# Heads and state written channel-major in column tiles: a Mamba block with a four-bit FFN on one core

## What is computed

```python
# u (16, 256, 256); all float32
z, xBC, dt = split(u @ W_in, [512, 1280])          # W_in (256, 1288)
xBC = silu(conv(xBC))                              # causal, 4 taps along the sequence, with bias
x, B, C = split(xBC, [512, 640])                   # x: 8 heads of 64 channels; state 128
dt = softplus(dt + dt_bias); A = -exp(A_log)       # one of each per head
y = ssd(x * dt, A * dt, B, C)                      # y_t = sum over s <= t of
                                                   #   exp(sum of A*dt over (s, t]) (C_t . B_s) dt_s x_s
y = (y + x * D) * silu(z)
y = y * rsqrt(mean(y^2) + 1e-5) * norm_scale
h = layernorm(u + y @ W_out)
g, v = h @ Wg.T, h @ Wu.T                          # 256 -> 2048, four-bit weights with a scale
out = layernorm(h + (gelu_tanh(g) * v) @ Wd.T)     # per 32 inputs; 2048 -> 256
```

## Time and profile before

| | |
|---|---|
| runs | 974.57, 980.9, 981.12 us; median 980.9 |
| profiled execution | 978.1 us, its span 976.4 us |
| mean granted TensorE clock | 0.969 of full speed |
| PE busy | 912.1 us (93%) |
| PEld busy | 795.8 us (82%) |
| DVE busy | 689.8 us (71%) |
| ACT busy | 528.8 us (54%) |
| POOL busy | 84.3 us (9%) |
| DMA | 23.28 MB, queues busy for 7.4% of 16 engines |

### The profile page before, as it was taken

One profiled execution on the slowest core, in us unless ns is written; L12 is line 12 of the kernel. 1 busy time (PEld: TensorE's weight loads), 2 busy tenths in 40 slices (PEclk: granted clock), 3 DMA queues, 4 the chain that ended last, 5 costly groups with the idle time before them and its releaser, 6 DMA issues.

```text
span 976.4 us, 16131 instructions
## 1 busy us (share of the span) xinstructions
PE 912.1 (93%) x5416; PEld 795.8 (82%) x5416; DVE 689.8 (71%) x1402; ACT 528.8 (54%) x1044; POOL 84.3 (9%) x170
## 2 busy tenths in 40 slices
PE   4678689899999999999999999999999999999997
PEld 3447679788897888878897889878898888888887
DVE  6766987786668775687658765687668775776453
ACT  4643477447634764447634664448645664455232
POOL 2110001200020001200021001200011001100000
PEclk9787879999999999999999999999999999999999
DMA  4011100010001000010001000010001000000000
GB/s 132 31 57 48 32 17 22 15 41 1 23 1 66 0 0 21 22 43 0 21 0 65 0 0 21 21 45 0 21 0 65 1 1 12 35 21 1 1 34 11
DMA packets 18813, 23.28 MB, mean 24 GB/s; under 512 B 1728, under 2 KB 15296, under 8 KB 18752
## 3 DMA queue, kind: packets, MB, share of 16 engines
q1 hardware_dynamic: 18176, 22.56, 7.1%
q10 hardware_dynamic: 576, 0.03, 0.0%
HBM read 14.19 MB, written 4.19 MB: 19 GB/s over the span
## 4 chain that ended last, share of the span: by engine, by line
issue 54%; PE 29%; DVE 8%; POOL 4%; ACT 2%; DMA 1%; POOLq 0%; DVEq 0%; SPq 0%; ACTq 0%
PE mixer L561 2%; PE up_bank L481 2%; PE down L481 2%; PE down L482 2%; PE down L483 2%; PE up_bank L483 2%; PE up_bank L482 2%; PE gate_bank L481 2%; PE gate_bank L483 2%; PE gate_bank L482 2%; DVE xbc L897 2%; PE mixer L481 2%; PE mixer L482 1%; PE mixer L483 1%; POOL rms L1131 1%
## 5 line engine op out<-in xcount | busy, mean ns | idle before, releaser
L481 PE MATMUL down<-wd_hi,in_hi 128*128 128x256 f32 x512 | 145.2, 284 | 0.7 <-DVE in_lo L1018 0.7
L482 PE MATMUL down<-wd_lo,in_hi 128*128 128x256 f32 x512 | 144.6, 282 | 0.0
L483 PE MATMUL down<-wd_hi,in_lo 128*128 128x256 f32 x512 | 144.3, 282 | 0.0
L897 DVE SCALAR_TENSOR_TENSOR xbc<-mixer,chan,xbc 128x510 f32<-128x510 f32 (+1 forms) x162 | 111.1, 686 | 28.3 <-ACT xbc L689 23.4
L767 ACT ACTIVATE act_sb<-gate_bank 128x512 f32<-128x512 f32 (+1 forms) x144 | 78.8, 547 | 82.7 <-PE gate_bank L483 81.5
L753 ACT ACTIVATE in_hi<-act_sb 128x512 fp32r<-128x512 f32 (+1 forms) x144 | 83.4, 579 | 68.9 <-PE down L483 55.6
L481 PE MATMUL up_bank<-hT_hi,wu_hi 128*128 128x512 f32 (+1 forms) x288 | 109.1, 379 | 11.1 <-DVE act_sb L1032 11.0
L481 PE MATMUL gate_bank<-hT_hi,wg_hi 128*128 128x512 f32 (+1 forms) x288 | 115.2, 400 | 4.5 <-DVE wg_lo L1085 4.5
L1032 DVE SCALAR_TENSOR_TENSOR act_sb<-up_bank,act_sb 128x512 f32<-128x512 f32 (+1 forms) x144 | 90.6, 629 | 37.6 <-PE up_bank L483 20.1
L483 PE MATMUL gate_bank<-hT_hi,wg_lo 128*128 128x512 f32 (+1 forms) x288 | 108.2, 376 | 0.0
L482 PE MATMUL gate_bank<-hT_lo,wg_hi 128*128 128x512 f32 (+1 forms) x288 | 107.6, 374 | 0.0
(11 more groups left out here) (205 smaller groups left out, 2008.5 us busy)
## 6 DMA issues: line engine op xcount, KB each, us to landing
xbc<-in_u_t_dram SPq DMA_DIRECT2D x7, 512.0 KB, 3.6
h_sb<-in_u_dram SPq DMA_DIRECT2D x7, 512.0 KB, 4.0
h_res<-h_sb SPq DMA_DIRECT2D x7, 512.0 KB, 3.4
out_dram<-h_res SPq DMA_DIRECT2D x7, 512.0 KB, 3.3
scales<-in_ffn_s_dram SPq DMA_DIRECT2D x24, 128.0 KB, 2.0
packed<-in_ffn_w_dram SPq DMA_DIRECT2D x8, 96.0 KB, 1.9
xbc<-in_u_t_dram SPq DMA_DIRECT2D x2, 256.0 KB, 2.7
xbc<-in_W_in_dram SPq DMA_DIRECT2D x1, 512.0 KB, 5.8
```

What stands on the lines that cost most here:

```text
L481: nc.tensor.matmul(dst, lh, rh, start=first, stop=False, skip_group_check=True)
L482: nc.tensor.matmul(dst, lh, rl, start=False, stop=False, skip_group_check=True)
L483: return nc.tensor.matmul(dst, ll, rh, start=False, stop=last, skip_group_check=True)
L897: ins = stt(acc[:, :, d:], src[:, :, 0:SEQ - d], chan[:, c:c + 1], acc[:, :, d:], ALU.mult, ALU.add)
```

## The change

Six things change together.

1. z is made channel-major like x: z_i is channel tile i of all tokens. The first and last group have four z steps of 256 tokens in place of two of 512 channels.
2. `Y` and `Yoff` are written channel-major. Per head, `xdt` (or `xtail`) of the head is now the stationary operand (64 columns) and `dec` (or C.B) moves (128 columns). Even heads write partitions 0 to 63 and odd heads partitions 64 to 127, each at a column tile of its own (`tile_position`).
3. The transposes `gT` are gone. ACT and DVE split the digits straight from `zs` (`g`). The squares are written out, folded twice on DVE and summed over partitions by a matmul of one column (`S`); one DVE and one POOL instruction make `rms`.
4. `e2` and its two matmuls in `CB` are gone. The state's decay comes from `E`: four matmuls of 512 columns over R behind `D1` and `D3`, in a bank of its own, and an exponential of 128 x 512 into `y`.
5. x*D is no longer made in `XT`. It is added in `Y` by four DVE instructions of 128 columns (`x_d`), straight from the channel-major x. So the next group's load of u, which overwrites x, waits for the last `x_d` and not for the last `XT`.
6. `x5` moves ahead of the FFN's first unit, `z2` and `z3` join the lists of the first and last group, and the lists of the weight preparation follow the new names.

```diff
 USES = { "full":
-   [..., "z3", "CB0", "XT0",
-    "D0a", "D0b", "Y0", "XT1", "D1a", "D1b", "Y1", "Yoff0", "CB1", "gT0", "XT2", "D2a", "D2b",
-    "op0", "gT1", "Y2", "XT3", "D3a", "D3b", "op1", "gT2", "Y3", "Yoff1", "op2", "gT3", "op3"],
+   [..., "z3", "CB0", "XT0",
+    "D0a", "D0b", "Y0", "XT1", "D1a", "D1b", "E0", "Y1", "Yoff0", "CB1", "XT2", "D2a", "D2b", "S0",
+    "op0", "Y2", "XT3", "S1", "D3a", "D3b", "E1", "op1", "Y3", "Yoff1", "S2", "op2", "S3", "op3"],
 SLOTS = { "full":
-   [[], ["x5", "x0", "z0"], ["x1", "z1"], ["x2", "z2"], ["x3", "z3"], ["CB0", "R0", "XT0"],
-    ["D0"], ["R1", "Y0", "XT1"], ["D1"], ["R2", "Y1", "CB1", "gT0", "XT2"], ["D2"],
-    ["R3", "op0", "gT1", "Y2", "XT3"], ["D3"], ["op1", "gT2", "Y3"], ["op2", "gT3"], ["op3", "ln1"], ["ln2"]],
+   [["x5"], ["x0", "z0"], ["x1", "z1"], ["x2", "z2"], ["x3", "z3"], ["CB0", "R0", "XT0"],
+    ["D0"], ["R1", "Y0", "XT1"], ["D1"], ["R2", "Y1", "CB1", "g0", "XT2"], ["D2", "S0"],
+    ["R3", "op0", "g1", "Y2", "XT3"], ["S1", "D3"], ["op1", "g2", "Y3"], ["S2", "op2", "g3"],
+    ["S3", "op3", "ln1"], ["ln2"]],
...
 # PE, CB
-                nc.tensor.matmul(b[:, 3 * P:3 * P + H], tri_r[:, :], dA_hi[:, 2 * i + 1, :], ...)
-                nc.tensor.matmul(b[:, 3 * P:3 * P + H], tri_r[:, :], dA_lo[:, 2 * i + 1, :], ...)
 # PE, behind D of an odd tile
+                use = f"E{i // 2}"
+                wait_bank(pe, use, g)
+                for a, rows in ((1, P), (0, HP)):
+                    for n, part in enumerate(R_of(g)):
+                        mm = nc.tensor.matmul(bank(g, use)[0:rows, :],
+                                              tri_r[:, P - 1:P].to_broadcast([P, rows]), part[:, a::2, :],
+                                              start=n == 0, stop=n == 1, skip_group_check=True)
 # PE, Y (and the same with xtail and cb[:, 1, :] for Yoff)
-                    mm = nc.tensor.matmul(bank(g, use)[:, h * HP:(h + 1) * HP], dec_of(g, i)[:, h, :],
-                                          xdt[:, h * HP:(h + 1) * HP], start=True, stop=True)
+                    j, a = h // 2, h % 2
+                    mm = nc.tensor.matmul(bank(g, use)[a * HP:(a + 1) * HP, j * P:(j + 1) * P],
+                                          xdt[:, h * HP:(h + 1) * HP], dec_of(g, i)[:, h, :],
+                                          start=True, stop=True, tile_position=(0, a * HP), skip_group_check=True)
-                    nc.tensor.matmul(bank(g, use)[:, :], cb[:, 1, :], xtail[:, :], start=True, stop=True)
-            elif kind == "gT":
-                for j in range(JT):
-                    mm = nc.tensor.transpose(bank(g, use)[:, j * P:(j + 1) * P],
-                                             zs[:, i, j * P:(j + 1) * P], ident[:, :])
+            elif kind == "S":
+                wait(pe, sq_sum, g, i + 1)
+                nc.tensor.matmul(bank(g, name)[:, 0:1], y[:, i % 2, 0:P], tri[:, P - 1:P], start=True, stop=True)
 # ACT
-                    nc.scalar.activation(e2[:, i // 2, :], bank(g, f"CB{i // 2}")[:, 3 * P:3 * P + H], ACT.Exp)
+                    nc.scalar.activation(y[:, 1, :], bank(g, f"E{i // 2}")[:, :], ACT.Exp)
-                nc.scalar.activation(y[:, i % 2, :], zs[:, i, :], ACT.Square, accum_out=ssq[:, i:i + 1])
-                nc.scalar.activation(gT_hi[:, :], bank(g, f"gT{i}")[:, :], ACT.Copy)
+                nc.scalar.activation(by_block(y[:, i % 2, :]), tile_of(zs, i), ACT.Square)
+                nc.scalar.activation(g_hi[:, :, :], tile_of(zs, i), ACT.Copy)
 # DVE, Y of an odd tile (of an even one: x_d from the bank, then the product with zs)
-                    tt(yc, bank(g, f"Y{i}")[:, :], yc, ALU.add)
-                    tt(head(xdt[:, :]), head(bank(g, use)[:, :]), e2[...], ALU.mult)
-                    tt(yc, yc, xdt[:, :], ALU.add)
+                    tt(yc, bank(g, f"Yoff{i // 2}")[:, :], yc, ALU.mult)
+                    x_d(yc, yc, i)
+                    tt(yc, bank(g, f"Y{i}")[:, :], yc, ALU.add)
 # DVE, XT and g
-                tt(head(y[:, i % 2, :]), head(bank(g, use)[:, :]), d_bc[...], ALU.mult)
-                tt(gT_lo[:, :], bank(g, f"gT{i}")[:, :], f32(gT_hi[:, :]), ALU.subtract)
+                tt(q[:, 0:2 * P], q[:, 0:2 * P], q[:, 2 * P:4 * P], ALU.add)
+                tt(q[:, 0:P], q[:, 0:P], q[:, P:2 * P], ALU.add)
+                tt(g_lo[:, :, :], tile_of(zs, i), f32(g_hi[:, :, :]), ALU.subtract)
+            elif kind == "S":
+                ts(rms_v[:, i:i + 1], bank(g, name)[:, 0:1], 1.0 / DI, 4 * EPS, ALU.mult, ALU.add)
+        def x_d(dst, src, i):
+            for j in range(JT):
+                at = (slice(None), slice(j * P, (j + 1) * P))
+                ins = stt(dst[at], xbc[:, j, i * P:(i + 1) * P], chan[:, 34 + j:35 + j], src[at], ALU.mult, ALU.add)
 # SP
-                wait_for((ready(g - 1, f"XT{tiles(g - 1) - 1}")[0], g - 1, ...))
+                wait_for((y_step, g - 1, D_ADDED[tiles(g - 1) - 1]))
                 sp.dma_start(u32[:, :, 0:width(g)], uT_of(g)).then_inc(uT_in.sem, 16)
```

More of the change, by code:

```diff
@@ L525, in mixer @@
                     wait(pe, xbc_ok, g, 2)
-                    wait(pe, dA_ok, g, 1)
                     b = bank(g, use)
@@ L580, in mixer @@
                     wait_bank(pe, use, g)
-                    wait(pe, gT_l, g, i + 1)
+                    wait(pe, g_l, g, i + 1)
                     for j in range(JT):
-                        mm = mm3(bank(g, use)[:, 0:DM], [x[:, j * P:(j + 1) * P] for x in (gT_hi, gT_lo)],
+                        mm = mm3(bank(g, use)[:, 0:DM], [x[:, j, :] for x in (g_hi, g_lo)],
                                  [w[:, j, :] for w in (wout_hi, wout_lo)], j == 0, j == JT - 1)
@@ L668, in tanh @@
                 wait(act, conv, g, 3 * n + 3)
-                wait(act, ssq_ok, g - 1, tiles(g - 1))
+                wait_ready(act, f"S{tiles(g - 1) - 1}", g - 1)
                 if n >= 2:
@@ L700, in mixer @@
                     wait_ready(act, f"z{i}", g)
-                    before = min(i, tiles(g - 1) - 1)
-                    wait_ready(act, f"gT{before}", g - 1)
-                    wait(act, ssq_ok, g - 1, before + 1)
-                    nc.scalar.activation(zs[:, i, :], bank(g, f"z{i}")[:, :], ACT.Tanh, scale=0.5)\
+                    wait(act, g_l, g - 1, tiles(g - 1))
+                    nc.scalar.activation(zs[:, i, 0:width(g)], bank(g, f"z{i}")[:, 0:width(g)], ACT.Tanh, scale=0.5)\
                         .then_inc(z_tanh.sem, 1)
                 elif kind == "CB":
-                    if tiles(g) == 2:
-                        tanh(CT - 1, g)
                     wait_ready(act, f"CB{i}", g)
@@ L721, in mixer @@
                 elif kind == "D":
-                    if i % 2 == 0:
-                        wait(act, cb_ok, g, i // 2 + 1)
-                        nc.scalar.activation(e2[:, i // 2, :], bank(g, f"CB{i // 2}")[:, 3 * P:3 * P + H],
-                                             ACT.Exp).then_inc(e2_ok.sem, 1)
                     if i == 0:
@@ L737, in mixer @@
                                              ACT.Exp).then_inc(dec_ok.sem, 1)
-                elif kind == "gT":
-                    wait(act, y_step, g, (3, 8, 11, 16)[i])
-                    nc.scalar.activation(y[:, i % 2, :], zs[:, i, :], ACT.Square,
-                                         accum_out=ssq[:, i:i + 1]).then_inc(ssq_ok.sem, 1)
-                    wait_ready(act, f"gT{i}", g)
+                    if i % 2:
+                        if i > 2:
+                            wait_ready(act, f"S{i - 2}", g)
+                        wait_ready(act, f"E{i // 2}", g)
+                        nc.scalar.activation(y[:, 1, :], bank(g, f"E{i // 2}")[:, :], ACT.Exp).then_inc(e_ok.sem, 1)
+                elif kind == "g":
+                    wait(act, y_step, g, Y_DONE[i])
+                    nc.scalar.activation(by_block(y[:, i % 2, :]), tile_of(zs, i), ACT.Square).then_inc(squared.sem, 1)
                     if i:
@@ L932, in mixer @@
                     wait_ready(dve, use, g)
-                    wait(dve, ssq_ok, g, i - 1)
-                    tt(head(y[:, i % 2, :]), head(bank(g, use)[:, :]),
-                       d_bc[:, :].unsqueeze(2).to_broadcast([P, H, HP]), ALU.mult).then_inc(y_step.sem, 1)
                     tt(head(xdt[:, :]), head(bank(g, use)[:, :]),
@@ L970, in mixer @@
-                    wait(dve, zs_ok, g, i + 1)
-                    tt(zs[:, i, :], zs[:, i, :], yc, ALU.mult).then_inc(y_step.sem, 1)
-                elif kind == "gT":
-                    wait(dve, gT_h, g, i + 1)
-                    tt(gT_lo[:, :], bank(g, f"gT{i}")[:, :], f32(gT_hi[:, :]), ALU.subtract).then_inc(gT_l.sem, 1)
+                    yc, s0 = y[:, i % 2, :], 6 * (i // 2)
+                    if i % 2 == 0:
+                        if i:
+                            wait_ready(dve, f"S{i - 2}", g)
+                        wait_ready(dve, f"Y{i}", g)
+                        x_d(yc, bank(g, f"Y{i}"), i)
+                    else:
```

(7 more changed lines are left out.)

180 lines of the change are left out of this document (86 added, 94 removed), and 18 rows, old and new, of tables (SLOTS, USES).

## The result

The changed kernel takes 955.6 us (median of 4 runs, 955.01 to 958.49), the kernel before 978.75 us beside it (median of 4, 974.57 to 981.12). The ratio is 0.9768, with a 95% interval of 0.974 to 0.9796: 23 us or 2.3% less. The forecast was 967 us, with a range from 958 to 1002. The sign was right, and the gain is larger than the range allowed.

What follows compares the result with a forecast made beforehand. PE was taken to bound the six full groups after group 0. Terms of -18.0, +1.2, +2 and +1 gave -13.8 us: 978.1 became 964.3 profiled, 967 us against the 980.9 median, range 958 to 1002.

Steps and rivals of the forecast that it cites:

- pairs of groups 1 to 6: PE's work per pair of tiles falls from 5.57 to 4.36 us, 1.2 us less for each pair outside the first group.
- the pause at the loop's head: DVE's 1.98 us ahead of unit 0 in a loop iteration, in which nothing holds it; no saving counted.
- group 0: Only half of the saving of its pairs was counted there, 1.2 us.
- first group: Order of waits decides; E and more z steps cost, Y1 and Yoff save 1 us: +2 us, between -1 and +4.
- last group and its FFN: No term of its own; its pair was among the 15 outside the first group, at -1.2 us each.
- thinner cover: DVE's cover before PE's up product in the slot of Y1 shrinks from 2.5 to 1 us: +1 over six groups.
- x5 first: In loop iterations unit 0 comes 2.4 us later, PE's wait for unit 1 shrinks: nothing, -0.5 to +0.5 us a group.
- the baseline: The profiled 978.1 us lie 2.8 us below the median, so the forecast was set against 980.9 us.
- Column tiles: In Y and Yoff, even and odd heads run side by side, 1.0 us a set (0.58); rival in turn, 1003 us (0.25).
- Drains: Rival: each of four changes a pair between full array and tiles costs 0.14 to 0.25 us: 975 to 982 us (0.17).
- DVE in the slot of `Y1`: Rival: DVE becomes late there if its small steps are 0.1 us dearer; 2 us a group return, about 975 us.
- SP, POOL, ACT: Their changed work was priced at nothing; the later load of u, at about 495 us, keeps 11 us of cover.

Runs made afterwards that it cites:

- e1: The kernel before with x5 moved ahead of the first unit in the full and last groups, nothing else changed: 975.3 us, ratio 0.9982.
- e2: The changed kernel with x5 put back in the slot of x0 and z0 in the full and last groups: 958.8 us, ratio 0.9789.
- e10: The kernel before with the edits of e1 and e5 together: 969.3 us, ratio 0.9918.
- e4: The changed kernel with heads ordered 0, 2, 4, 6, 1, 3, 5, 7 in Y and Yoff, so most neighbours share a column tile: 971.7 us, ratio 0.9927.
- e7: The changed kernel with the odd tile's transposes put between the head pairs of the even tile's Y, eight array changes instead of two: 972.2 us, ratio 0.9918.
- e5: The kernel before with 48 long-past waits (24 instructions, no work) added at DVE's start, shifting its code: 972.1 us, ratio 0.9921.
- e6: The changed kernel with 120 long-past waits (60 instructions, no work) added at DVE's start: 963.0 us, ratio 0.9832.

## Why the prediction was off

The forecast of -13.8 us and the measured -23.1 us, term by term. The middle column is what the prediction's own step gave; the right one is from the profiled executions.

| term | forecast | measured |
|---|---|---|
| pairs of groups 1 to 6 | -14.4 | -12.35 (2.12 + 4 x 2.08 + 1.91) |
| the pause at the loop's head | 0 | -7.2 (4 x 1.81) |
| group 0 | -1.2 | -3.5 |
| first group | +2 | 0 |
| last group and its FFN | -1.2 | 0 (+0.66 - 0.67) |
| thinner cover | +1 | 0 |
| sum | -13.8 | -23.1 |

**The step that failed** is "x5 first", with the row it rests on. It read the pause of the earlier trace rows as a fixed feature, "1.98 us in which nothing holds it", in either order of the work, and priced the part at "nothing, between -0.5 and +0.5 us a group". On x5 itself that was right (`e1`, `e2`, `e10`). What it left out is that this pause hangs on where DVE's code lies, in four of five iterations, so that a change that moves DVE's instructions may end it or begin it. It was worth 7.2 us of the 9.3 by which the terms were off, and without it the 955.6 would have been 962.8, inside the range. Put back, it would make a loop group 106.46 + 1.81 = 108.3 us, the upper end of the 107.7 to 108.3 that the prediction named. The other terms were off by 1 to 2.3 us each and nearly cancel, which is luck. The last 2 us of the 11.4 between 967 and 955.6 are the baseline: the prediction added 2.8 us for the distance from the profiled execution to the median, and it came to 0.6, before and after. The sign was not to be had from the trace; but the term was. The spread of 110.35 against 108.33 and 108.43 in groups with the same work, and an idle time that no semaphore ended, are both in it. As a case of its own (pause gone in four iterations at its 1.8 us: 7 us less than the 967) it would have taken the low end of the range from 958 to 951, past the 955.6 measured.

**Column tiles** were right, on the step on which the forecast hung. A set takes 0.92 to 1.03 us where 1.0 was taken, and `e4` shows that this hangs on neighbours in different tiles. Added up from start to start over one full group (the one ahead of the last), `Y` fell from 6.92 to 3.90 us, `Yoff` with `CB` and the running sums of `e2` went from 3.08 to 3.36, the transposes' 1.73 are gone, `E` costs 1.86, `S` 0.56. That is -2.05 a group or -1.02 a pair, against the -1.2 forecast and the 1.04 of the loop. `S` was dearer in the forecast (0.44 a pair, measured 0.28), `gT` too (0.98, measured 0.87). `op` rose from 5.63 to 6.08 us a group, for which I have no cause, and other steps gave 0.3 back.

**Drains**: a change has a price, 0.157 us in `e7`, inside the 0.14 to 0.25 of the rival; none was seen where `E` changes its form, and that it is the array emptying is not shown. What was wrong there was to set it on top of the sets: the changes in and out of the sets of a pair are part of the measured 0.92 to 1.03. The forecast's "about 0.1 us for a start and an end that nothing overlaps" had held most of it.

**DVE in the slot of `Y1`** was not late. Its steps:

```profile
452.51 0.69 DVE L965 TENSOR_TENSOR y<-mixer,y 128x512 f32<-128x512 f32 x1 [1.14 <-PE mixer L583]
453.24 1.14 DVE L1002 SCALAR_TENSOR_TENSOR y<-xbc,chan,y 128x128 f32<-128x128 f32 x4
454.41 0.69 DVE L969 TENSOR_TENSOR y<-mixer,y 128x512 f32<-128x512 f32 x1
...
458.61 0.68 DVE L1049 SCALAR_TENSOR_TENSOR act_sb<-up_bank,act_sb 128x512 f32<-128x512 f32 x1
```

`x_d` takes 454.41 - 453.24 = 1.17 us where 0.85 was taken from the 0.20 of `cb`; why one of its instructions is dearer was not looked into. From the first of these rows to the end of the unit it is 6.8 us where 6.6 were counted. The up product begins about 460.3, so the cover is 1.0 us as forecast, and no wait of PE came of it. The 2 us a group of this rival did not come, although `x_d` was some 0.3 us dearer.

**First group.** `Y1` and `Yoff` took 2.77 and 1.81 us before. After:

```profile
52.91 1.09 PE L573 MATMUL mixer<-act_sb,xdt 128*64 128x128 f32 x16 [0.91 <-issue]
53.80 1.07 PE L583 MATMUL mixer<-cb,xtail 128*64 128x128 f32 x16
...
59.64 0.56 PE L590 MATMUL mixer<-tri,y 128*128 128x1 f32 x2 [3.48 <-DVE y L978]
```

They take 0.89 and 1.01 us, 2.7 less and not 1 less; the mean granted clock in 30:75 rose from 0.80 to 0.84. Against that stand `E`'s 1.0 and the new wait of 3.48 us for the folded squares, and it came out even. **Group 0** gained 3.5 us where 1.2 was counted. In `e2`, without x5 first, it still gained 2.6, so x5 is not the main reason; the granted clock of 120:150 was higher after (0.89 to 0.90 against 0.77 to 0.78). With x5 first groups 0 and 1 together took from 0.7 (`e10` against `e5`) to 5.3 us less (the changed kernel against `e2`), most of it with the clock. DVE is busy for 19 of 20 us in 110:130, so PE does not set the pace there, and no run separates the parts further.

**SP, POOL, ACT.** The load of u went from 78.7 to 90.4 us behind its group's cut (issued at 482.38; the forecast's 495 is 93.5 behind the cut) and is first used at 497.00; nothing waits for it. None of the three brought PE a new wait in the loop.

## What to carry to other kernels

Ask of an idle time that no semaphore ended where it recurs. If it stands at the head of a hardware loop and not in its first iteration, suspect that it depends on where the code lies, and try it as here: shift the engine's code by instructions that do nothing, and count the fetches. An edit made for another reason can switch such a pause on or off, so compare the lengths of loop groups with and without it before crediting a change. Column tiles paid here only with neighbours in PE's order in different tiles (`e4`) and the sets kept whole: each change from the full array to the tiles or back cost 0.16 us (`e7`). Here DVE's mis-sized steps did no harm to the forecast, since they were covered; the unexplained pause in it did.

## What the runs showed of the hardware that I had not expected

- A pause of 1.8 to 2.0 us of DVE at the head of a loop iteration goes or comes with 24 or 60 instructions ahead of the loop, and with it come five 8 KB fetches on q14 an iteration. It was worth 7.2 us in groups 2 to 5 of the kernel before (110.35 against 108.55 in `e5`) and 5.4 in those of `e6`.
- Plain float32 matmuls of 128 columns in two column tiles start in pairs, a pair every 0.11 us, when the tiles alternate. With four heads in a row in one tile they start 0.11 us apart singly, and overlap, at 0.05 us, only where one tile's run meets the other's (`e4`).
- A change between full array and column tile cost 0.157 us among transposes and heads (twelve more in a group: 1.89 us), and nothing to be seen between the float32r matmuls of `E` (starts 0.23 to 0.24 us apart).
- After the same wait of 3.6 us the granted clock was 0.50 over the next ten microseconds in two variants and 0.94 in the changed kernel; after waits in the last group it was 0.61, 0.72 or 1.00. These dips go with 1 to 4 us each and stand beside, not in, the effect under test.
